# Causal mask of the exponentials: GpSimd selects in SBUF for TensorE mask matmuls, six casts moved to ScalarE, and a turn table written anew

## The chip, the cores and the metric

The kernel runs on 1 core of one Trainium2 chip. The metric is the device time of one execution in microseconds (us); the times of before are from 3 runs. TensorE is PE in the profile (PEld its weight loads), VectorE is DVE, ScalarE is ACT, GpSimd is POOL, and SP is the engine that issues most of the DMAs.

## What is computed

One transformer layer over 32 sequences (B) of 512 tokens (T) with 256 features, in float32: attention with rotary positions and a causal mask, then a mixture of experts. Cut to the attention that the change touches:

```python
q = (x @ Wq + bq).reshape(b, t, 16, 16).transpose(0, 2, 1, 3)      # 16 heads of 16
k = (x @ Wk + bk).reshape(b, t, 4, 16).transpose(0, 2, 1, 3)       # 4 groups, 4 heads each
v = (x @ Wv + bv).reshape(b, t, 4, 16).transpose(0, 2, 1, 3)
q, k = _rope(q), _rope(jnp.repeat(k, 4, axis=1)); v = jnp.repeat(v, 4, axis=1)
scores = jnp.einsum('bhtd,bhsd->bhts', q, k) / 4.0
scores = jnp.where(jnp.tril(jnp.ones((t, t), dtype=bool)), scores, -jnp.inf)
attn = jnp.einsum('bhts,bhsd->bhtd', jax.nn.softmax(scores, axis=-1), v)
out = attn.transpose(0, 2, 1, 3).reshape(b, t, 256) @ Wo + bo
```

Around it stand layer norms and residual sums. The second half routes each token to 2 of 16 experts (a gate of 16 outputs, top 2), adds a shared expert, and normalises again.

## The kernel before

The program has two phases. `attention_phase` does the attention, the gate and the routing of all 32 sequences and scatters each token's row to its experts' lists in DRAM; `expert_phases` then works through the 286 tiles of these lists and at last through the 32 sequences for the shared expert. The change is in the first phase alone.

The attention phase is a software pipeline over turns (`TURNS`, c from -3 to 33). In the turn c, sequence c has its exponentials and its weighing, c+1 has its first row maxima, c+2 its projections, its rotation and its splits, and c-1 and c-2 their output projection, norms, gate and routing. Within a turn everything has its place in a grid (g, e): four groups g of heads, and in each eleven units e of exponentials (`EXP_UNITS`). `turn_order()` walks this grid and puts next to every unit what the tables name there: `MAX_AT` and `SUMS_AT` place the maxima (step M) and the weighing (step P), `MISC` places steps of several engines, and `SIDE` places steps of one engine. Every engine walks the same list, takes its own steps from it and does them strictly in that order; semaphores tie the engines together.

Scores are made twice. For the maxima (`score_max`, L733), TensorE multiplies a query block by the keys up to the diagonal, with 96 rows in bfloat16: each float32 number is split into three bfloat16 parts, and the parts are stacked in `qs` and `ks`. A matmul of the identity with `mask_max` (L735) adds -3e38 above the diagonal, and VectorE takes the negated maximum of each row (L967). For the exponentials (`score_exp`, L749), TensorE multiplies keys by queries, with three more rows that subtract the maximum, and a matmul of the identity with `mask_exp` (L751) adds -3e38 to the 128x128 block on the diagonal, once for every head and key block. Units go through three PSUM buffers (`ps_a`). ScalarE takes the exponential of each unit into `probs` in SBUF (L856). `weigh` (L763) then multiplies them by the values and by ones, with all four heads of a group side by side in `ps_out`; key block j=0 and j=1 are weighed in the group itself, j=2 and j=3 in the next one. VectorE transposes the sums (L1005), inverts the denominators (L1007), and GpSimd divides (L677).

The splits of a sequence are GpSimd's: `split(b, unit, stage)` for unit 0 and 1 (the two halves of the queries) and 2 (the keys). Stage 0 forms the rotated number in `rest` (L598, L600, L602) from what VectorE left in `roped_q` (L979) and `roped_k`; stages 1 and 2 each round `rest` to a bfloat16 part (a cast written as an addition of zero, L594) and subtract that part (L596). There is one `rest`, so the units follow each other. When a unit is split, SP stores its three parts in DRAM (`store_parts`, L472), and when all are stored it loads them back as stacks, first the keys (L479) and then the queries of the four groups (L483), which `score_max` of the first group waits for in the next turn. The first sequence's splits are made by VectorE (`first_split`).

GpSimd also does three `root` steps a turn (eight small dependent operations each), two `split_max`, four `divide` and eight indirect DMAs that scatter rows (L666), all in one queue.

## Time and profile before

| | us |
|---|---|
| median of 3 runs | 2591.48 |
| lowest and highest | 2581.96, 2599.78 |
| profiled execution, its own time | 2595.59 |
| span of that execution (first to last instruction) | 2593.8 |
| attention phase, about | 0 to 1850 |
| expert tiles | 1855 to 2385 |
| shared expert and last norm | 2385 to 2594 |

The times below are from the profiled execution, and counted from its first instruction. A row of the timeline gives the start, the duration, the engine, the line and operation, output and inputs, and in brackets how long the engine had been idle and what ended that. A matmul's duration holds its way through the array, so two matmuls overlap, and what one costs is read from the distance between two starts. The values step (L881, one each sequence) is used as the mark of a turn: from one of its starts to the next.

### The profile page before, as it was taken

The page shows a single profiled execution, that of the slowest core. Times are in us where ns is not written, and L with a number is a line of the kernel's source. Part 1 is how long each engine was busy: PE and PEld are TensorE (multiplying, and loading weights), DVE is VectorE, ACT ScalarE, POOL GpSimd, SP SyncE. Part 2 cuts the span into 40 slices and gives each one's busy share as a digit, 9 for nine tenths or more (in the row PEclk, how much of TensorE's full clock was granted, in tenths as well). Part 3 has the DMA queues.
Part 4 walks back from the last instruction along what each step waited for, and adds up shares of the span by engine and source line. Part 5 has one row for each costly group of instructions (what it writes and reads, how often), then busy time and mean ns, then how long its engine had stood idle before and what let it go on. Part 6 is the DMA issues. An engine that isn't in the chain of part 4 may idle for free. (4 is left out here: it accounts for less than half of the span.)

```text
span 2593.8 us, 59479 instructions
## 1 busy us (share of the span) xinstructions
PE 2344.7 (90%) x18030; PEld 1507.9 (58%) x18030; DVE 2031.0 (78%) x5412; ACT 1396.6 (54%) x3228; POOL 1704.4 (66%) x2889
## 2 busy tenths in 40 slices
PE   4899999999999998899999999995389999999997
PEld 2555555555555555555555555553268877877664
DVE  5788888888887888788888878884357777776887
ACT  1455666556665665565666656564134444444664
POOL 2556767667766776677677667644266666766887
PEclk7899999999999998999999999997689999999999
DMA  4345444554455443455444453331356556554997
GB/s 126 89 135 148 128 130 148 155 150 134 131 156 159 128 130 111 124 151 163 139 128 136 137 155 116 115 116 58 81 153 182 155 148 198 162 150 147 318 348 243
DMA packets 288649, 387.93 MB, mean 150 GB/s; under 512 B 27922, under 2 KB 238098, under 8 KB 288212
## 3 DMA queue, kind: packets, MB, share of 16 engines
q1 hardware_dynamic: 260788, 308.56, 40.6%
q0 software_dynamic: 27552, 75.57, 8.6%
q8 instruction: 155, 2.54, 0.4%
q14 instruction: 154, 1.26, 0.2%
HBM read 193.40 MB, written 172.27 MB: 141 GB/s over the span
## 5 line engine op out<-in xcount | busy, mean ns | idle before, releaser
L856 ACT ACTIVATE probs<-ps_a 128x512 f32<-128x512 f32 (+1 forms) x1408 | 716.3, 560 | 519.0 <-PE ps_a L751 459.1
L967 DVE TENSOR_REDUCE negmax<-ps_d 128x2 f32<-128x768 f32 (+3 forms) x768 | 779.7, 1033 | 155.8 <-PE ps_d L735 142.3
L733 PE MATMUL ps_d<-ks,qs 96*128 96x128 bf16 (+3 forms) x2048 | 494.9, 308 | 97.0 <-DMA qs<-q_stack_dram 49.1
L749 PE MATMUL ps_a<-qs,ks 99*128 99x512 bf16 (+3 forms) x2048 | 526.3, 305 | 16.7 <-ACT probs L856 8.7
L735 PE MATMUL ps_d<-mask_max,ident_bf 128*128 128x128 bf16 x2048 | 401.3, 224 | 0.0
L751 PE MATMUL ps_a<-mask_exp,ident_bf 128*128 128x128 bf16 x2048 | 392.2, 221 | 0.0
L733 PEld LDWEIGHTS ps_d<-ks,qs 96*128 96x128 bf16 x2048 | 204.7, 100 | 267.5 <-issue 113.0
L1378 POOL DMA_INDIRECT y_dram<-ysb,to_row x286 | 282.4, 987 | 118.2 <-issue 81.5
L763 PE MATMUL ps_out<-probs,va 128*32 128x512 f32 (+3 forms) x4096 | 335.5, 446 | 0.2 <-ACT probs L856 0.2
L749 PEld LDWEIGHTS ps_a<-qs,ks 99*128 99x128 bf16 x2048 | 200.4, 98 | 217.1 <-issue 66.0
L1451 PE MATMUL ps_gu<-wgu,rows_t 128*128 x1144 | 305.7, 391 | 10.2 <-issue 6.7
L666 POOL DMA_INDIRECT sorted_dram<-h,slot x256 | 255.8, 999 | 65.8 <-issue 64.9
L1542 ACT ACTIVATE gate<-ps_gu 128x128 f32<-128x128 f32 x286 | 79.6, 278 | 269.2 <-issue 136.3
L751 PEld LDWEIGHTS ps_a<-mask_exp,ident_bf 128*128 128x128 bf16 x2048 | 202.8, 99 | 28.4 <-issue 21.5
L1451 PEld LDWEIGHTS ps_gu<-wgu,rows_t 128*128 128x128 f32 x1144 | 201.2, 196 | 29.0 <-issue 12.5
L735 PEld LDWEIGHTS ps_d<-mask_max,ident_bf 128*128 128x128 bf16 x2048 | 205.4, 100 | 0.4 <-issue 0.3
L1465 PE MATMUL ps_y<-wd,hid_t 128*128 x572 | 181.5, 399 | 19.0 <-ACT hid_t L1548 17.4
L763 PEld LDWEIGHTS ps_out<-probs,va 128*32 128x32 f32 x4096 | 108.1, 110 | 143.9 <-issue 74.7
L1611 DVE TENSOR_TENSOR hid<-ps_gu,gate 128x128 f32<-128x128 f32 x286 | 83.3, 291 | 117.4 <-ACT gate L1542 98.8
L205 POOL TENSOR_TENSOR pool_cell<-zero_col 1x1 f32<-1x1 f32 x318 | 58.7, 185 | 173.7 <-DVE slot L1101 111.9
L677 POOL TENSOR_TENSOR heads<-by_token,inverse 128x256 f32<-128x256 f32 x128 | 80.8, 631 | 135.5 <-DVE inverse L1007 129.4
L786 PE MATMUL ps_d<-wo,headst 128*128 128x256 f32 x512 | 148.2, 440 | 11.0 <-DVE place L1086 8.9
(196 smaller groups left out, 4447.4 us busy)
## 6 DMA issues: line engine op xcount, KB each, us to landing
qs<-q_stack_dram SPq DMA_DIRECT2D x128, 384.0 KB
rows<-sorted_dram SPq DMA_DIRECT2D x286, 129.0 KB
y_in<-y_dram SPq DMA_DIRECT2D x32, 1024.0 KB
q_stack_dram<-q_parts SPq DMA_DIRECT2D x64, 384.0 KB
x_in<-in_x SPq DMA_DIRECT2D x32, 512.0 KB
q_stack_dram<-q_parts SPq DMA_DIRECT2D x64, 256.0 KB
x<-in_x SPq DMA_DIRECT2D x32, 512.0 KB
h_dram<-h SPq DMA_DIRECT2D x32, 512.0 KB, 3.8
```

Source lines behind the costliest of these rows:

```text
L666: pool.indirect_dma_start(out=sorted_dram[b // (B // 2)][:, :], in_=h2[:, k, j, :], in_offset=None, out_offset=bass.IndirectOffsetOnAxis(a ...
L733: pe.matmul(ps_d[:, number % 2, at:at + width], qs[0:KR, b % 2, h, j * P:(j + 1) * P], ks[0:KR, b % 2, g, 0:width], start=True, stop=False)
L735: ins = pe.matmul(ps_d[:, number % 2, at + j * P:at + (j + 1) * P], ident_bf[:, :], mask_max[:, :], start=False, stop=True)
L749: pe.matmul(ps_a[:, number % 3, at:at + width], ks[0:KM, b % 2, g, j * P:(j + 1) * P], qs[0:KM, b % 2, g * HG + h0 + k, j * P:T], start=Tr ...
L751: ins = pe.matmul(ps_a[:, number % 3, at:at + P], ident_bf[:, :], mask_exp[:, :], start=False, stop=True)
L763: ins = pe.matmul(ps_out[32 * h:32 * h + 32, j * P:T], va[:, b % 3, j, g * 32:(g + 1) * 32], probs[:, at:at + width], start=(j == 0), stop ...
L786: ins = pe.matmul(ps[:, k * D:(k + 1) * D], headst[:, c, j * P:(j + 1) * P], wo[:, c, :], start=(c == 0), stop=(c == NC - 1))
L856: act.activation(probs[:, at:at + nh * width], ps_a[:, number % 3, 0:nh * width], ACT.Exp) \
L967: dve.tensor_reduce(negmax[:, g // 2, j, at:at + nh], src, AX_X, ALU.max, negate=True) \
L1378: pool.indirect_dma_start(out=y_dram[:, :], in_=ysb[:, k, :], in_offset=None, out_offset=bass.IndirectOffsetOnAxis(ap=to_row[k][:, 0:1].bi ...
L1451: ins = pe.matmul(ps_gu[:, t % 2, 0:2 * I], rows_t[:, t % 2, c, :], wgu[:, expert[t], c, :], start=(c == 0), stop=(c == NC - 1))
L1465: pe.matmul(ps_y[:, t % 2, 0:D], hid_t[:, t % 2, :], wd[:, expert[t], :], start=True, stop=True) \
```

## The change

`score_exp` no longer issues the mask matmul, and `mask_exp` is gone. In its place GpSimd gets a step `Z` for each group and key block, 16 in a turn: `triangle` waits until the last unit of that block has its exponentials, and sets to zero, in place in `probs`, the entries whose query stands before the key in the four heads' 128x128 diagonal blocks (one instruction over 4x128 columns). `weigh` waits for that step and not for the exponentials. In `split`, the six casts of a turn are taken from GpSimd and done by ScalarE as copies with rounding (`cast`); `rest` and the parts then pass from GpSimd to ScalarE and back by the same counting semaphore. The tables of the turn are new.

```diff
 MISC = {
     (0, 1): [("xt", 0, 2)],
-    (0, 8): [("W", 3, -1), ("R", 1, -1)],
-    (0, 9): [("cn", 0, -2)],
-    (1, 0): [("op", 0, -1)],
-    (1, 2): [("op", 1, -1)],
...
+    (0, 5): [("Z", 0, 0), ("T", 3, -1)],
+    (0, 6): [("Z", 15, -1), ("cn", 0, -2)],
...
+    (0, 10): [("op", 0, -1)],
+    (1, 0): [("op", 1, -1)],
+    (1, 1): [("Z", 3, 0)],
...
-MAX_AT = [[0, 0, 1, 4, 6, 10], [1, 2, 3, 6, 9, 9], [0, 2, 4, 5, 6, 8], [1, 2, 4, 7, 8, 9]]
-SUMS_AT = [10, 5]
+MAX_AT = [[0, 0, 1, 3, 9, 10], [3, 3, 5, 9, 9, 9], [0, 2, 3, 5, 8, 9], [2, 2, 5, 6, 7, 8]]
+SUMS_AT = [10, 4]
...
+    "cast0b": (1, 10),
+    "cast0c": (2, 1),
+    "cast1b": (3, 2),
+    "cast1c": (3, 4),
+    "cast2b": (3, 9),
+    "cast2c": (3, 10),
...
                 if stage or unit or b >= 1:
                     steps.settle()
-                if stage == 1 and unit == 0 and b >= 1:
-                    pool.wait_ge(parts_stored[(b - 1) % 2], PER_STORE * ((b - 1) // 2 + 1))
                 if stage:
                     k = stage - 1
-                    steps.did(pool.tensor_tensor(parts[k], r, zero_col[0:n, :].to_broadcast([n, T]), ALU.add))
-                    steps.settle()
                     steps.did(pool.tensor_tensor(parts[2] if k == 1 else r, r, parts[k], ALU.subtract))
...
+            def triangle(b, g, j):
+
+                pool.wait_ge(a_taken, A_NO["E", (g, LAST_OF_J[j]), b] + 1)
+                width = T - j * P
+                own = probs[:, PROBS_AT[j]:PROBS_AT[j] + HG * width].rearrange("p (h w) -> p h w", h=HG)[:, :, 0:P]
+                pool.affine_select(out=own, in_=own, compare_op=ALU.is_ge, fill=0.0, base=0,
+                                   pattern=[[0, HG], [1, P]], channel_multiplier=-1).then_inc(triangled, 1)
...
-                    pe.matmul(ps_a[:, number % 3, at:at + width], ks[0:KM, b % 2, g, j * P:(j + 1) * P],
-                              qs[0:KM, b % 2, g * HG + h0 + k, j * P:T], start=True, stop=False)
-                    ins = pe.matmul(ps_a[:, number % 3, at:at + P], ident_bf[:, :], mask_exp[:, :],
-                                    start=False, stop=True)
+                    ins = pe.matmul(ps_a[:, number % 3, at:at + width], ks[0:KM, b % 2, g, j * P:(j + 1) * P],
+                                    qs[0:KM, b % 2, g * HG + h0 + k, j * P:T], start=True, stop=True)
                 ins.then_inc(a_full, 1)
 
             def weigh(b, g, j):
 
-                pe.wait_ge(a_taken, A_NO["E", (g, LAST_OF_J[j]), b] + 1)
+                pe.wait_ge(triangled, Z_NO["Z", HG * g + j, b] + 1)
...
+            def cast(b, unit, k):
+
+                n = G * DH if unit == 2 else P
+                part = k_parts[:, k, :] if unit == 2 else q_parts[:, unit, k, :]
+                if unit == 0 and k == 0 and b >= 1:
+                    act.wait_ge(parts_stored[(b - 1) % 2], PER_STORE * ((b - 1) // 2 + 1))
+                act.wait_ge(split_steps, SPLITS * (3 * b + unit) + 2 * k + 1)
+                act.copy(part, rest[0:n, :]).then_inc(split_steps, 1)
```

The code of the changed kernel is some lines longer, so its lines have other numbers: 750 and 752 are the maxima's matmul and mask, 766 the exponentials' matmul, 801 the output projection, 603 the subtractions, 605, 607 and 609 the three `rest`, 616 the select, 692 the division, 909 the cast.

TensorE's queue of before, where a turn comes to the first maxima of the next sequence (group 0, ahead by one turn); L786 is the output projection:

```order
L786 MATMUL ps_d<-wo,headst 128x256 x4
L749 MATMUL ps_a<-qs,ks 128x512
L751 MATMUL ps_a<-mask_exp,ident_bf 128x128
L733 MATMUL ps_d<-ks,qs 128x128
L735 MATMUL ps_d<-mask_max,ident_bf 128x128
```

And of the changed kernel, at the same first maxima:

```order
L801 MATMUL ps_d<-wo,headst 128x256 x4
L766 MATMUL ps_a<-qs,ks 128x512
L801 MATMUL ps_d<-wo,headst 128x256 x4
L766 MATMUL ps_a<-qs,ks 128x512 x3
L750 MATMUL ps_d<-ks,qs 128x128
L752 MATMUL ps_d<-mask_max,ident_bf 128x128
```

In before, the first maxima come after one half of the output projection and one unit of exponentials, and the other half comes two sets of maxima later; now both halves and all four 512-wide units stand ahead of them. What follows is in both an ordinary row of maxima and units up to the query projection (L779, now L794).

GpSimd's queue of before, at the end of a sequence's splits (L594 and L596 on `k_parts` are the keys' casts and subtractions, L677 the division, L205 the wait for the scatter):

```order
L677 TENSOR_TENSOR heads<-by_token,inverse 128x16x16
L594 TENSOR_TENSOR k_parts_negmax_t<-rest,zero_col 64x512
L596 TENSOR_TENSOR rest<-rest,k_parts_negmax_t 64x512
L594 TENSOR_TENSOR k_parts_negmax_t<-rest,zero_col 64x512
L596 TENSOR_TENSOR k_parts_negmax_t<-rest,k_parts_negmax_t 64x512
L677 TENSOR_TENSOR heads<-by_token,inverse 128x16x16
L205 TENSOR_TENSOR pool_cell<-zero_col 1x1
```

And of the changed kernel, from the keys' `rest` on:

```order
L609 TENSOR_TENSOR rest<-roped_k_v_t 64x512
L616 AFFINE_SELECT probs<-probs 128x4x128
L692 TENSOR_TENSOR heads<-by_token,inverse 128x16x16
L603 TENSOR_TENSOR rest<-rest,k_parts_negmax_t 64x512
L603 TENSOR_TENSOR k_parts_negmax_t<-rest,k_parts_negmax_t 64x512
L616 AFFINE_SELECT probs<-probs 128x4x128 x2
L616 AFFINE_SELECT probs<-probs 128x512
L616 AFFINE_SELECT probs<-probs 128x4x128
L692 TENSOR_TENSOR heads<-by_token,inverse 128x16x16
L616 AFFINE_SELECT probs<-probs 128x4x128
L219 TENSOR_TENSOR pool_cell<-zero_col 1x1
```

The keys' casts are gone from this queue; one select stands inside the keys' split, and five stand behind it, ahead of the scatter, where before there was one division.

ScalarE's queue of the changed kernel at the same place (L883 to L891 are the gate's, L923 the norm of a sequence's input, L909 the casts of the keys):

```order
L883 ACTIVATE logits_t<-ps_a,act_bias 128x128
L871 ACTIVATE probs<-ps_a 128x384
L871 ACTIVATE probs<-ps_a 128x512 x2
L888 ACTIVATE gates<-ps_a 128x64
L891 ACTIVATE gates<-gates,act_bias 128x64
L909 CAST k_parts_negmax_t<-rest 64x512
L923 ACTIVATE h<-x_in,shift,rstd 128x256 x2
L871 ACTIVATE probs<-ps_a 128x512
L909 CAST k_parts_negmax_t<-rest 64x512
L923 ACTIVATE h<-x_in,shift,rstd 128x256 x2
```

In before the same stretch has no cast, and the four norms stand in one piece. Between the two casts of the keys there are now two norms and an exponential.

## Rows read from the trace of the kernel before

**Rows 1.** Busy time by stage: length, PE, PEld, DVE, ACT, POOL, clock, DMA share, GB/s.

```profile
200.00:1650.00 1450.00, 1368.57 (x12361) 813.33 (x12360) 1237.53 (x2881) 877.55 (x1806) 1013.09 (x1680) 0.98 0.47 138
1366.15:1418.42 52.27, 49.86 (x461) 29.55 (x459) 45.69 (x107) 32.56 (x68) 37.17 (x63) 1.00 0.47 138
1418.42:1472.62 54.20, 51.19 (x461) 30.75 (x459) 45.56 (x107) 32.56 (x68) 37.18 (x63) 0.97 0.44 133
973.37:1035.74 62.37, 55.28 (x461) 32.87 (x459) 53.53 (x137) 32.78 (x68) 40.21 (x64) 0.89 0.38 116
```

**Rows 2.** The values step of all sequences, from the view of its line.

```profile
L881 ACT COPY va<-ps_a x32: 372/378/379, 24.7 to 1689.5; 128x256 f32<-128x256 f32 x32
```

**Rows 3.** Timeline, TensorE: exponentials' matmuls and their masks.

```profile
1012.00 0.22 PE L749 MATMUL ps_a<-qs,ks 99*128 99x128 bf16 x1
1012.06 0.22 PE L751 MATMUL ps_a<-mask_exp,ident_bf 128*128 128x128 bf16 x1
1012.12 0.22 PE L749 MATMUL ps_a<-qs,ks 99*128 99x128 bf16 x1
```

**Rows 4.** Timeline: from first maxima over the splits to the next sequence's, and on.

```profile
1335.13 0.22 PE L733 MATMUL ps_d<-ks,qs 96*128 96x128 bf16 x1 [1.53 <-DMA qs<-q_stack_dram]
...
1347.04 1.27 POOL L598 TENSOR_TENSOR rest<-roped_q 128x512 f32<-128x512 f32 x1 [1.93 <-issue]
...
1375.74 1.15 POOL L596 TENSOR_TENSOR k_parts_negmax_t<-rest,k_parts_negmax_t 64x512 bf16<-64x512 f32 x1
1376.92 1.93 SPq L472 DMA_DIRECT2D k_stack_dram<-k_parts_negmax_t  x3
1380.70 0.34 SPq L479 DMA_DIRECT2D ks<-k_stack_dram  x1
1387.46 0.22 PE L733 MATMUL ps_d<-ks,qs 96*128 96x128 bf16 x1 [1.69 <-DMA qs<-q_stack_dram]
...
1388.88 1.98 PE L786 MATMUL ps_d<-wo,headst 128*128 128x256 f32 x8
...
1393.64 1.93 PE L779 MATMUL ps_d<-h1t,wq 128*128 128x512 f32 x4
```

**Rows 5.** Who waited for whom in the turn 1366.15 to 1418.42: GpSimd's waits (us, times, longest).

```profile
POOL heads L677 <- DVE inverse L1007: 3.8, 1, 3.8
POOL pool_cell L205 <- DVE slot L1101: 3.3, 1, 3.3
POOL rest L598 <- issue: 1.9, 1, 1.9
POOL var L632 <- issue: 0.8, 1, 0.8
```

**Rows 6.** Timeline, GpSimd: casts and subtractions of one unit.

```profile
1403.72 1.05 POOL L594 TENSOR_TENSOR q_parts<-rest,zero_col 128x512 bf16<-128x512 f32 x1
1404.85 1.17 POOL L596 TENSOR_TENSOR rest<-rest,q_parts 128x512 f32<-128x512 f32 x1
```

**Rows 7.** Timeline, GpSimd: selects over 128 columns, iotas over 16 and 512.

```profile
2.38 0.29 POOL L556 TENSOR_SCALAR_AFFINE_SELECT ident_bf<-ident_bf 128x128 bf16<-128x128 bf16 x1
2.63 0.29 POOL L559 TENSOR_SCALAR_AFFINE_SELECT mask_max<-mask_max 128x128 bf16<-128x128 bf16 x1
...
3.38 0.14 POOL L567 IOTA iota_e<- 128x16 f32 x1
...
1849.68 0.57 POOL L1367 IOTA own_row<- 128x512 f32 x1 [12.41 <-POOLq L336]
```

**Rows 8.** Groups of the whole span: a copy and the exponentials of ScalarE.

```profile
L885 ACT COPY h1t<-ps_a 128x512 f32<-128x512 f32 x64 | 37.6, 590 | 2.3 <-PE ps_a L803 2.3
L856 ACT ACTIVATE probs<-ps_a 128x512 f32<-128x512 f32 (+1 forms) x1408 | 716.3, 560 | 519.0 <-PE ps_a L751 459.1
```

**Rows 9.** GpSimd's cast, from the view of its line: shortest, median, longest in ns.

```profile
L594 POOL TENSOR_TENSOR q_parts<-rest,zero_col x124: 1032/1041/1367, 56.6 to 1688.6; 128x512 bf16<-128x512 f32 x124
```

More of the change, by code:

```diff
@@ L293, in layer @@
         mask_max = sb("mask_max", [P, P], BF16)
-        mask_exp = sb("mask_exp", [P, P], BF16)
         before = sb("before", [P, P], BF16)
@@ L325, in attention_phase @@
         v[n] for n in ("wq", "wkv", "bq", "bk", "rope", "wo", "bo", "gate_w", "act_bias", "wgu", "wd"))
-    (ident, ident_bf, mask_max, mask_exp, before, ones_bf, iota_e, token) = (
-        v[n] for n in ("ident", "ident_bf", "mask_max", "mask_exp", "before", "ones_bf", "iota_e", "token"))
+    (ident, ident_bf, mask_max, before, ones_bf, iota_e, token) = (
+        v[n] for n in ("ident", "ident_bf", "mask_max", "before", "ones_bf", "iota_e", "token"))
     (h2_std, h2_mean, counts, pool_cell, dve_cell, zero_col, tile_no, row_no) = (
@@ L560, in _ @@
                                base=0, pattern=[[-1, P]], channel_multiplier=1).then_inc(consts, 1)
-            pool.affine_select(out=mask_exp[:, :], in_=mask_exp[:, :], compare_op=ALU.is_ge, fill=MASKED,
-                               base=0, pattern=[[1, P]], channel_multiplier=-1).then_inc(consts, 1)
             pool.affine_select(out=before[:, :], in_=before[:, :], compare_op=ALU.is_ge, fill=1.0,
@@ L690, in _ @@
                         divide(b, arg)
+                    if step == "Z" and exists(b):
+                        triangle(b, arg // HG, arg % HG)
                     if step != "side":
@@ L907, in _ @@
                     if step == "side":
+                        if exists(c + 2) and c + 2 > 0:
+                            for unit in range(3):
+                                for k in range(2):
+                                    if at == SIDE[f"cast{unit}" + "bc"[k]]:
+                                        cast(c + 2, unit, k)
                         for part in range(2):
```

63 lines of the change are left out of this document (26 added, 37 removed), and 19 rows, old and new, of the table MISC.

## The prediction

> **What bounds the kernel now.** I read the busy time by stage first, then the timeline of one turn, then who waited for whom, and last the prices.
>
> The change is in the attention phase, whose turns run from one values step to the next: 31 intervals between 24.7 and 1689.5 us [rows 2]. A quiet turn is 52.27 us long and has TensorE at its full clock; another is 54.20 us at 0.97, and one of the two in which VectorE plans the experts' tiles is 62.37 us [rows 1]. In the quiet turn TensorE shows 49.9 us busy, VectorE 45.7, ScalarE 32.6 and GpSimd 37.2 [rows 1]. TensorE's figure says least: a matmul's record is 0.22 us long where the next starts after 0.06 [rows 3].
>
> So the reader should look for what makes TensorE stop. It stops once in every turn, at the first maxima of the next sequence, for the load of the query stacks: 1.53 us in one turn and 1.69 in the next [rows 4]. From there one can walk round a loop. First maxima at 1335.13; the query projection 6.2 us later (1387.46 to 1393.64 in the next turn); `rest`, when VectorE has rotated, at 1347.04, that is 5.7 us after the projection began; GpSimd's splits of queries and keys up to 1376.89 (29.8 us); SP's key store at once, the key load at 1380.70, and the first maxima again at 1387.46 (10.6 us) [rows 4]. The sum is 52.3 us, the turn itself. GpSimd waits for something 9.8 us in a turn, but all of it lies behind the keys' last subtraction and ahead of `rest` (the waits before the division, the scatter, the root and `rest` itself [rows 5]): inside its 29.8 us of the loop it never stops. The turn is set by this loop, and TensorE and VectorE are nearly as long.
>
> **The change part by part.**
>
> The mask matmuls. Matmul, mask and matmul start 0.06 us apart (1012.00, 1012.06, 1012.12 [rows 3]). There are 64 masks of the exponentials in a turn, so TensorE gets rid of 64 x 0.0585 = 3.7 us a turn, and of 2048 x 0.0585 = 120 us in all. That is the most that this part can bring, 125 us if the slower stretches are counted.
>
> GpSimd's queue. Its occupied time now is 52.3 - 9.8 = 42.5 us a turn. A cast and the wait behind it take 1.13 us (1403.72 to 1404.85 [rows 6]); six go: -6.7. Sixteen selects over 4x128 columns come, and no row shows one. A select over 128 columns takes 0.29 us, and two start 0.25 apart; an iota over 16 columns takes 0.14 us and one over 512 takes 0.57 [rows 7]. If the select has the short iota's fixed part of 0.13, its columns cost 0.157 us per 128, and one over 512 lasts 0.13 + 4 x 0.157 = 0.76 us and holds the queue for some 0.72. From below it is the long iota's 0.57 us (0.53 held), from above four times the short select's 0.29, 1.15 us (1.11 held). I take 0.72, since it rests on the select's own row; 16 x 0.72 = 11.5. For the second cast of the keys nothing stands between the two subtractions in GpSimd's queue, so GpSimd waits for ScalarE: 0.6 us for the cast and some 0.6 for what ScalarE is in the middle of, 1.2 in all. GpSimd then has 42.5 - 6.7 + 11.5 + 1.2 = 48.5 us (45.5 to 54.8 between the ends) of occupied time in a turn.
>
> The loop. From the first maxima to the query projection, half an output projection (1.8 to 2.0 us [rows 4]), two 512-wide units and a pair of maxima have been moved ahead of the maxima, and three masks are gone: 6.2 becomes about 3.2. Rotation stays at 5.7. In GpSimd's piece six casts go (-6.7), nine of the sixteen selects stand in it (9 x 0.72 = +6.5), and the wait for the last cast comes in (+1.2): 29.8 becomes 30.8. The stores and loads keep their 10.6, the same DMAs in the same order behind the same last subtraction. Sum: 3.2 + 5.7 + 30.8 + 10.6 = 50.3 us (48.6 and 53.8 with the select at its two ends). That is also what GpSimd's 48.5 needs, with some 1.8 us left for the waits which today are 9.8.
>
> ScalarE. A copy of 512 columns out of PSUM is 0.59 us [rows 8]; out of SBUF I take the same, 0.6, between half and twice that. Six are 3.6 us on an engine with 32.6 of 52.3 busy, and hide beside its waits for matmuls (459 us in the run, over 32 sequences some 14 a turn [rows 8]). But its queue is in order too. Behind a cast that waits for GpSimd stand exponentials, and behind these, three PSUM buffers later, TensorE. Where that cover is gone, a GpSimd that is late by 1 us makes TensorE late by nearly 1 us.
>
> The new wait of `weigh`. It waited for an exponential and now waits for a select behind whatever GpSimd has queued. The hardest place is key block 3 of group 0: its select stands behind the four scatters and a `split_max`. The counting step `cn` has been moved ahead by three units, so the scatters may start that much earlier, and the waits before the division and the scatter (3.8 and 3.3 us [rows 5]) are where the five added selects of that place go. I cost this at nothing; if that cover is gone the price is that of a select, 0.7 us, once or twice in a turn.
>
> The shared port. GpSimd's cast has a shortest time of 1032 ns, a median of 1041 and a longest of 1367 [rows 9]: in the middle case it loses 9 ns to anyone else. The Trainium skill ("SBUF — State Buffer", on the shared port pair) says that VectorE and GpSimd share a pair of SBUF ports and that whichever starts first keeps it for the whole instruction while the other is blocked. By that rule a select that meets one of VectorE's additions of two SBUF operands would stand still for up to that addition's length, and 16 selects give it 16 more chances; by the row such meetings are rare, and I add nothing. At the longest cast's excess of 0.33 us on every one of nine selects the loop would be 3 us longer, which is the case without gain below.
>
> The rest. The expert phases are untouched. The first three turns and the two of the planner are bounded otherwise and I give them the same gain, for want of a better row.
>
> The sum: 52.3 - 50.3 = 2.0 us, less a little, x 31 intervals = 60 us. The profiled execution took 2595.6 us (its span 2593.8) and would take 2535.6; the median of the runs is 4.1 lower, so the forecast is 2531.
>
> **The rivals.**
>
> Everything is gained. The loop gets its full relief because ScalarE's casts return in time and a select is as short as an iota, and the turn falls by all 3.7 us that TensorE loses: 2591.5 - 31 x 3.7 = 2477. For it speaks that VectorE's 45.7 us [rows 1] would fit into a turn of 48.6; against it that VectorE would then be busy 94% of the time, where it is now 87%, with the same two buffers between it and TensorE.
>
> No gain. The loop keeps its length, because each of the casts inside the splits comes back late (0.3 us more at six places is 1.8), or because selects are held up. Then TensorE's 3.7 us become waiting at the same place: 2580 to 2592, say 2586. For it speaks that the bound engine now is not the one that is relieved; against it the 3 us that were taken out between maxima and projection.
>
> The clock. Turns of 54.2 us have TensorE at a mean of 0.97 against 1.00 in the quiet ones of 52.3 [rows 1], and such a stretch follows the wait for the query stacks. About half of the turns have one. If TensorE, with 3.7 us less to do, idled more and every turn had one, some 14 more turns would lose 1.9 us each: 2531 + 27 = 2558. The Trainium skill ("TensorE: Matmul & The Clock Gate", the part on the oscillation) describes that: an idle TensorE has its clock halved until it has been busy again. The trace agrees in that the clock falls to the 1.2 GHz level after such a wait. Against it speaks that the first maxima now come later in the turn, so that this longest wait should shrink.
>
> Slower: GpSimd becomes the bound. Without its selects it has 37.0 us, and it can't do without some 1.3 us of waiting. With a held time s of one select the turn is 38.3 + 16 s, so it is as long as today's at s = 0.87 us; above that the kernel is slower. With s = 1.0, four short selects of 0.25 us one after the other, the turn is 54.3 and the time 2591.5 + 31 x 2.0 = 2654; at the upper end of 1.11 it is 56.1 and 2710. For it: a pattern of two dimensions in SBUF is in no row. Against: the per-column price would have to be that of the whole instruction.
>
> **How the numbers follow.** Chances: my forecast 0.45, everything gained 0.14, no gain 0.18, the clock 0.07, GpSimd the bound 0.16. The likeliest is 2531. The range is 2472 to 2625: down to the full gain and a little more, up into the case of a bound GpSimd, leaving out its dear half and some of the others' edges. Of 1% (26 us, about what a measurement of this kernel can tell from no change): faster by more holds the forecast but for its upper edge, the full gain and the clock, 0.65; within 1% the case without gain and that edge, 0.19; slower 0.16.
>
> **What would show it.** In the profile of the changed kernel: no line of `mask_exp`, and 64 matmuls fewer a turn; the select's group with a mean near 0.76 us (over 0.9 and the slower case is on); the distance of two values steps near 50.3 us in quiet turns; GpSimd with under 3 us of waits a turn; from the first maxima to the projection about 3.2 us; from `rest` of the first query half to the keys' last subtraction about 31. I am wrong if GpSimd still waits 6 us or more in a turn while the turn is 52, for then the loop is held elsewhere; or if TensorE's weight loads for `weigh` begin to wait for the selects by more than 1 us a turn, for then the new wait, which I cost at nothing, is the bound.

## The result: 6% slower, and the profile after

| | us |
|---|---|
| kernel before, median of 4 runs beside it | 2590.75 |
| changed kernel, median of 4 runs | 2745.47 (2741.59 to 2747.52) |
| ratio, 95% interval | 1.0595 [1.0557, 1.0634] |
| predicted | 2531 (2472 to 2625) |

The change costs 155 us where 60 less were forecast. The line of the values step dates the loss. It gives shortest, median and longest time in ns, then its first and last start:

```profile
L896 ACT COPY va<-ps_a x32: 372/372/373, 23.9 to 1827.3; 128x256 f32<-128x256 f32 x32
```

From first to last it is 1803.4 us, against 1664.8 before [rows 2]: 138.6 of the 146 us by which the spans differ. So all but a few of the lost microseconds lie in the turns of the attention phase. Two turns of the changed kernel, columns as in [rows 1]:

```profile
1536.86:1594.97 58.11, 48.83 (x396) 26.46 (x396) 45.69 (x107) 35.87 (x73) 40.66 (x72) 0.97 0.41 124
1594.97:1653.03 58.06, 48.79 (x396) 26.42 (x396) 45.73 (x107) 35.87 (x73) 40.64 (x72) 0.97 0.41 124
```

The turn has grown from 52.3 to 58.1 us and is nearly constant, but no engine has more than 49 us in it. VectorE's 45.7 is what it was; GpSimd is busy 40.6, so it isn't the bound by its load. A turn that is long, regular and full of gaps is held by waits. Who waited for whom, whole span:

```profile
ACT probs L871 <- PE ps_a L766: 431.1, 308, 5.7
PEld ps_out L778 <- POOL probs L616: 336.1, 210, 7.9
DVE negmax L996 <- PE ps_d L752: 308.6, 179, 10.3
PE ps_out L778 <- POOL probs L616: 233.2, 153, 7.6
POOL probs L616 <- ACT probs L871: 182.1, 102, 6.7
...
POOL rest L603 <- ACT q_parts L909: 96.7, 34, 3.9
```

TensorE waits 233 us for the selects, some 7 us a turn, in `weigh` (L778); before, its matmuls waited 0.2 us there in all, for exponentials. VectorE's wait for TensorE's maxima has more than doubled (142.3 before). On the other side the wait at the first maxima for the query stacks, which closed the loop that I walked [rows 4], is not among the waits any more. TensorE's waits for selects in the second of the two turns above (us, times, longest):

```profile
PE ps_out L778 <- POOL probs L616: 7.3, 5, 3.5
```

One place shows how it comes. This is the timeline of the changed kernel about group 2 of a turn; the columns are start, duration, engine, line and so on, as before:

```profile
1641.71 0.22 PE L752 MATMUL ps_d<-mask_max,ident_bf 128*128 128x128 bf16 x1
...
1642.92 0.64 POOL L616 TENSOR_SCALAR_AFFINE_SELECT probs<-probs 128x512 f32<-128x512 f32 x1
...
1643.48 1.23 DVE L996 TENSOR_REDUCE negmax<-ps_d 128x2 f32<-128x1024 f32 x1
...
1644.78 0.25 POOL L631 TENSOR_TENSOR negmax_parts<-negmax,zero_heads 128x32 bf16<-128x32 f32 x1 [0.64 <-DVE negmax L996]
...
1645.96 1.23 POOL L616 TENSOR_SCALAR_AFFINE_SELECT probs<-probs 128x512 f32<-128x512 f32 x2
1646.65 0.85 PE L778 MATMUL ps_out<-probs,va 128*32 128x384 f32 x8 [3.50 <-POOL probs L616]
...
1648.09 1.58 ACT L871 ACTIVATE probs<-ps_a 128x512 f32<-128x512 f32 x3 [3.00 <-PE ps_a L766]
1648.69 0.31 PE L750 MATMUL ps_d<-ks,qs 96*128 96x128 bf16 x1
1648.80 0.31 PE L752 MATMUL ps_d<-mask_max,ident_bf 128*128 128x128 bf16 x1
...
1649.79 0.69 DVE L996 TENSOR_REDUCE negmax<-ps_d 128x4 f32<-128x512 f32 x1 [4.47 <-PE ps_d L752]
...
1650.24 1.16 POOL L603 TENSOR_TENSOR rest<-rest,q_parts 128x512 f32<-128x512 f32 x1 [3.06 <-ACT q_parts L909]
```

Read it as a circle. TensorE issues the last maxima of the next sequence's group 1 at 1641.71. VectorE is then in the middle of the rotation of the keys, and reduces them from 1643.48 to 1644.71. GpSimd's `split_max` needs that reduction and starts at 1644.78. Behind `split_max` in GpSimd's queue stands the select of group 2, key block 1 (the first of the two at 1645.96), and TensorE's second weighing from there, which only some 1.2 us of other work parts from those very maxima, needs this select: it starts at 1646.65 after 3.50 us of idling. In that time TensorE feeds nobody: ScalarE then stands 3.00 us, VectorE 4.47, and GpSimd itself 3.06, since its next cast stands in ScalarE's queue behind the late exponentials. And TensorE comes back with matmuls that start 0.11 us apart (1648.69, 1648.80) where it is 0.06 at the full clock [rows 3]: it is at the lower of its two levels, 1.2 GHz, for a while. The select of 1642.92 belongs to key block 2, which is needed later: the two stand in the wrong order, with the division and `split_max` between them.

### The profile page after: what moved, and what is told of

The parts are those of the page before. It is cut to its first block and busy times, and to the rows that moved or that the text cites. A ratio compares the mean times of both kernels' runs of the same rounds, so it can differ in the third digit from the quotient of the medians.

```text
span 2739.9 us, 55925 instructions
## 1 busy us (share of the span) xinstructions
PE 2287.1 (83%) x15982; PEld 1385.0 (51%) x15982; DVE 2037.5 (74%) x5412; ACT 1497.6 (55%) x3414; POOL 1819.9 (66%) x3213
## 5 line engine op out<-in xcount | busy, mean ns | idle before, releaser
L778 PE MATMUL ps_out<-probs,va 128*32 128x512 f32 (+3 forms) x4096 | 362.9, 453 | 233.4 <-POOL probs L616 233.2
L750 PE MATMUL ps_d<-ks,qs 96*128 96x128 bf16 (+3 forms) x2048 | 510.1, 318 | 48.6 <-issue 19.1
L766 PE MATMUL ps_a<-qs,ks 99*128 99x512 bf16 (+3 forms) x2048 | 482.3, 315 | 14.8 <-ACT h1t L900 7.6
L616 POOL TENSOR_SCALAR_AFFINE_SELECT probs<-probs 128x512 f32<-128x512 f32 x512 | 323.4, 640 | 184.9 <-ACT probs L871 182.1
L752 PE MATMUL ps_d<-mask_max,ident_bf 128*128 128x128 bf16 x2048 | 418.0, 232 | 0.0
L778 PEld LDWEIGHTS ps_out<-probs,va 128*32 128x32 f32 x4096 | 96.1, 110 | 419.6 <-POOL probs L616 336.1
L766 PEld LDWEIGHTS ps_a<-qs,ks 99*128 99x128 bf16 x2048 | 172.6, 99 | 227.0 <-issue 113.5
L1633 DVE COPY rows_t<-ps_t 128x256 f32<-128x256 f32 x286 | 118.9, 416 | 43.9 <-PE ps_t L1468 36.0
L1661 DVE SCALAR_TENSOR_TENSOR ysb<-ps_y,rows,half_row 128x256 f32<-128x256 f32 x286 | 138.4, 484 | 9.4 <-remote 4.7
L1468 PE MATMUL ps_t<-ident,rows 128*128 128x128 f32 x572 | 112.1, 279 | 31.4 <-DMA rows<-sorted_dram 31.4
L801 PE MATMUL ps_d<-wo,headst 128*128 128x256 f32 x512 | 126.0, 390 | 14.4 <-DVE headst L1043 10.6
```

Of the source, the lines that this page charges most:

```text
L616: pool.affine_select(out=own, in_=own, compare_op=ALU.is_ge, fill=0.0, base=0, pattern=[[0, HG], [1, P]], channel_multiplier=-1).then_inc( ...
L750: pe.matmul(ps_d[:, number % 2, at:at + width], qs[0:KR, b % 2, h, j * P:(j + 1) * P], ks[0:KR, b % 2, g, 0:width], start=True, stop=False)
L752: ins = pe.matmul(ps_d[:, number % 2, at + j * P:at + (j + 1) * P], ident_bf[:, :], mask_max[:, :], start=False, stop=True)
L766: ins = pe.matmul(ps_a[:, number % 3, at:at + width], ks[0:KM, b % 2, g, j * P:(j + 1) * P], qs[0:KM, b % 2, g * HG + h0 + k, j * P:T], st ...
L778: ins = pe.matmul(ps_out[32 * h:32 * h + 32, j * P:T], va[:, b % 3, j, g * 32:(g + 1) * 32], probs[:, at:at + width], start=(j == 0), stop ...
L1468: ins = pe.transpose(ps_t[:, t % 2, c * P:(c + 1) * P], rows[:, t % RD, c * P:(c + 1) * P], ident[:, :])
```

## The experiments

Chips differ: the kernel before ran at 2585 to 2595 us beside some of these kernels and at 2557 to 2567 beside others. So kernels are compared by the ratio to before on their own chip, and "turn" is the median distance of two values steps in the profiled run. Absolute times in the expectations are for a chip on which before takes 2591. One and the same kernel, order_only and best_order below, came out at 0.9863 on one chip and at 0.9787 on another, so a difference of under a point between kernels of different chips says little.

### Is it the wait, the load, the casts or the order?

**a_no_select.** The changed kernel without its selects (the causal mask of the probabilities is left out).

```diff
-                    if step == "Z" and exists(b):
-                        triangle(b, arg // HG, arg % HG)
...
-                pe.wait_ge(triangled, Z_NO["Z", HG * g + j, b] + 1)
+                pe.wait_ge(a_taken, A_NO["E", (g, LAST_OF_J[j]), b] + 1)
```

> The changed kernel without its selects: weigh waits for the exponentials as in before, and neither mask matmul nor select is left, so the causal mask of the probabilities is left out. Theory W (weigh's new wait behind GpSimd's in-order queue closes a ring of waits through TensorE and ScalarE): the turn falls from 58.1 us to 49 to 51 and the time to 2470 to 2540. Theory C (the six casts in ScalarE's queue hold the ring): the time stays above 2690. Theory T (the new tables are bad by themselves): it stays above 2690.

Measured: ratio 0.986 [0.9775, 0.9946], turn 51.3 us. The selects with their wait cost the whole loss and more, 7.3 points.

**a_scratch.** The same (mask left out again), but GpSimd does two small dependent products at each select's place, and nobody waits for them.

```diff
-                width = T - j * P
-                own = probs[:, PROBS_AT[j]:PROBS_AT[j] + HG * width].rearrange("p (h w) -> p h w", h=HG)[:, :, 0:P]
-                pool.affine_select(out=own, in_=own, compare_op=ALU.is_ge, fill=0.0, base=0,
-                                   pattern=[[0, HG], [1, P]], channel_multiplier=-1).then_inc(triangled, 1)
+                number = 2 * Z_NO["Z", HG * g + j, b]
+                for k in range(2):
+                    pool.wait_ge(triangled, number + k + 1)
+                    pool.tensor_tensor(other[:, :], other[:, :], other[:, :], ALU.mult).then_inc(triangled, 1)
...
-                pe.wait_ge(triangled, Z_NO["Z", HG * g + j, b] + 1)
+                pe.wait_ge(a_taken, A_NO["E", (g, LAST_OF_J[j]), b] + 1)
```

> As a_no_select, but at each select's place GpSimd does, after the same wait for the exponential, two small dependent products on a tile of its own (about 0.6 us together, as long as a select is held), which nobody waits for. The causal mask of the probabilities is left out. Theory W (the wait of weigh is the cost): close to a_no_select, at most 40 us above it. Theory L (GpSimd's load, or its own new waits for ScalarE's exponentials, is the cost): near the changed kernel, above 2680.

Measured: 0.9911 [0.9885, 0.9938], turn 53.2. Two products take some 0.64 us, as one select does. GpSimd's load so costs some 0.5 points against a_no_select, with intervals that overlap. What is left, 6.8 of 7.3, comes with TensorE's wait.

**a_casts_pool.** The changed kernel with the six casts back on GpSimd.

```diff
+                    steps.did(pool.tensor_tensor(parts[k], r, zero_col[0:n, :].to_broadcast([n, T]), ALU.add))
+                    steps.settle()
...
-                                    if at == SIDE[f"cast{unit}" + "bc"[k]]:
-                                        cast(c + 2, unit, k)
```

> The changed kernel with the six casts back on GpSimd, its tables and its selects kept. Theory C (casts on ScalarE are the harm, GpSimd waits for them some 5 us a turn): falls below 2650. Theory W: GpSimd's queue gets 6.7 us longer and loses 5 us of waiting, so the selects come as late as before or later: 2740 to 2850.

Measured: 1.0993 [1.0902, 1.1084], turn 61.5. Moving the casts helps the changed kernel by 4 points.

**order_only.** The kernel before with the new tables `MISC`, `MAX_AT`, `SUMS_AT` and `SIDE` (entries for selects and casts have no effect there). Masks on TensorE, casts on GpSimd. Two of the tables:

```diff
-MAX_AT = [[0, 0, 1, 4, 6, 10], [1, 2, 3, 6, 9, 9], [0, 2, 4, 5, 6, 8], [1, 2, 4, 7, 8, 9]]
-SUMS_AT = [10, 5]
+MAX_AT = [[0, 0, 1, 3, 9, 10], [3, 3, 5, 9, 9, 9], [0, 2, 3, 5, 8, 9], [2, 2, 5, 6, 7, 8]]
+SUMS_AT = [10, 4]
```

> The kernel before with the tables of the changed one: mask matmuls on TensorE, casts on GpSimd, no selects, only the order of the turn is new. Theory T (the order is the harm): above 2690. Theory W and C: within 40 us of before, 2550 to 2630.

Measured: 0.9863 [0.9779, 0.9946], turn 51.6 where before's median is 53.5. The new order by itself is a gain, as large as that of a_no_select.

**b_no_mask.** The kernel before without the mask matmuls of the exponentials, the mask left out.

```diff
-                    pe.matmul(ps_a[:, number % 3, at:at + width], ks[0:KM, b % 2, g, j * P:(j + 1) * P],
-                              qs[0:KM, b % 2, g * HG + h0 + k, j * P:T], start=True, stop=False)
-                    ins = pe.matmul(ps_a[:, number % 3, at:at + P], ident_bf[:, :], mask_exp[:, :],
-                                    start=False, stop=True)
+                    ins = pe.matmul(ps_a[:, number % 3, at:at + width], ks[0:KM, b % 2, g, j * P:(j + 1) * P],
+                                    qs[0:KM, b % 2, g * HG + h0 + k, j * P:T], start=True, stop=True)
```

> The kernel before with the 64 mask matmuls of the exponentials in each turn simply left out, so the causal mask of the probabilities is left out; order, casts and waits as before. It prices what the masks cost TensorE there. Theory N (TensorE's mask time is not on the path: two kernels that differ only by these masks, with the new order, both had turns of 51.3 to 51.4 us): 2560 to 2592 us, turn 51.5 to 52.3. Theory M (the masks' 3.7 us a turn are fully on the path, as in my case of everything gained): 2460 to 2490 us, turn near 48.6.

Measured: 0.9992 [0.9965, 1.002]. TensorE's 2048 masks are worth nothing there. A turn, and the wait for the query stacks in the whole run, which was 49.1 us in 23 turns before:

```profile
1422.30:1474.77 52.47, 47.07 (x396) 25.69 (x395) 45.82 (x107) 32.68 (x69) 37.52 (x63) 1.00 0.46 137
```

```profile
PE ps_d L733 <- DMA qs<-q_stack_dram: 55.4, 25, 3.2
```

TensorE is busy 47.1 instead of 49.9 us in a turn as long as before, and the wait that closes the loop is longer by 6 us in the whole run. This is what one expects where a loop through other engines sets the turn.

**select_alone.** The kernel before with only the selects in place of the masks, each put behind its exponentials, casts on GpSimd. The first lines of what is added to before's `MISC`; the other groups are alike:

```diff
+    (0, 0): [("Z", 14, -1)],
-    (0, 1): [("xt", 0, 2)],
+    (0, 1): [("Z", 15, -1), ("xt", 0, 2)],
...
+    (0, 6): [("Z", 0, 0)],
...
-    (0, 9): [("cn", 0, -2)],
-    (1, 0): [("op", 0, -1)],
+    (0, 9): [("Z", 1, 0), ("cn", 0, -2)],
+    (1, 0): [("Z", 2, 0), ("op", 0, -1)],
+    (1, 1): [("Z", 3, 0)],
```

> The kernel before with the selects in place of the mask matmuls and nothing else: before's order of turns, the casts on GpSimd, each select put into GpSimd's order two or three units behind the last exponential that it needs. GpSimd would have 42.5 + 16 x 0.62 = 52.4 us of occupied time in a turn of 52.3. Theory W (weigh waiting for a select in GpSimd's in-order queue sets the turn): 2680 to 2850 us, with waits of TensorE for the selects of over 4 us a turn. Theory P (the selects only hurt at the places that the new order gave them): 2590 to 2640 us.

Measured: 1.0974 [1.0921, 1.1027], turn 61.9. Without the new order and the casts the selects cost nearly 10%. Theory P is out: the damage isn't tied to one table. In its turn GpSimd has 46.7 us busy, 6 more than in the changed kernel; how much of this loss is its load and how much TensorE's wait is not shown.

**order_casts.** The new order and the casts on ScalarE, masks on TensorE, no selects: the edit of a_no_select, and

```diff
-                    ins = pe.matmul(ps_a[:, number % 3, at:at + width], ks[0:KM, b % 2, g, j * P:(j + 1) * P],
-                                    qs[0:KM, b % 2, g * HG + h0 + k, j * P:T], start=True, stop=True)
+                    pe.matmul(ps_a[:, number % 3, at:at + width], ks[0:KM, b % 2, g, j * P:(j + 1) * P],
+                              qs[0:KM, b % 2, g * HG + h0 + k, j * P:T], start=True, stop=False)
+                    ins = pe.matmul(ps_a[:, number % 3, at:at + P], ident_bf[:, :], mask_exp[:, :],
+                                    start=False, stop=True)
```

> The changed kernel with the masks back as TensorE matmuls and without the selects: the new order and the six casts on ScalarE alone. weigh waits for the exponentials. The new order alone took 2549 us with a turn of 51.4. Theory G (GpSimd's piece of the loop still sets the turn there, so 6.7 us less casts on it shorten the turn): 2480 to 2525 us. Theory V (with the new order VectorE, 46 of 51 us busy, and its hand-over with TensorE are the bound, and the casts bring nothing more): 2535 to 2560 us.

Measured: 0.9922 [0.9896, 0.9947], turn 52.5. A turn of it:

```profile
1404.72:1457.20 52.48, 49.58 (x460) 29.83 (x459) 47.02 (x108) 35.58 (x75) 30.90 (x57) 1.00 0.45 137
```

GpSimd is down to 30.9 us busy in a turn, and it is no faster than the order alone. The casts help only a GpSimd that has the selects too. Theory G is out: with the new order the loop through GpSimd's splits doesn't set the turn any more. That VectorE, 47.0 of 52.5 us busy, does is what theory V says and fits the time, but no run made VectorE's work shorter.

### Which place

**after_swap.** The changed kernel with two pairs of selects exchanged in `MISC`; the rows (1, 3) and (1, 6) are the edit of group 1, the rows (2, 8) and (3, 1) that of group 2.

```diff
-    (1, 3): [("Z", 5, 0)],
+    (1, 3): [("Z", 4, 0)],
-    (1, 6): [("Z", 4, 0), ("T", 0, 0), ("qe", 0, 2), ("qe", 1, 2)],
+    (1, 6): [("Z", 5, 0), ("T", 0, 0), ("qe", 0, 2), ("qe", 1, 2)],
-    (2, 8): [("Z", 10, 0), ("kk", 0, 2), ("W", 1, 0)],
+    (2, 8): [("Z", 9, 0), ("kk", 0, 2), ("W", 1, 0)],
-    (3, 1): [("Z", 9, 0)],
+    (3, 1): [("Z", 10, 0)],
```

> The changed kernel with two pairs of selects exchanged in GpSimd's order: those of group 1, key blocks 0 and 1, and those of group 2, key blocks 1 and 2. In the changed kernel the later-needed one stands first in each pair and waits for its exponentials while the other, whose exponentials are done and which TensorE waits for, stands behind it. If this head-of-line waiting makes the ring long: 2600 to 2700 us. If the length of GpSimd's queue ahead of the select (root, splits, division) is what matters and not these two places: 2730 to 2750 us.

Measured: 1.0023 [1.0005, 1.0042], turn 53.5. Four entries exchanged in a table give back nearly all of the 6%.

**swap_g1** and **swap_g2**, each with the edit of one group.

> The changed kernel with only one pair of selects exchanged in GpSimd's order: group 1, key blocks 0 and 1. Both pairs exchanged took 2601 us against 2745. Theory R (one ring: the place by group 2 sets the turn, since the chain of waits walked in the changed kernel goes through group 2's block 1 and not through this one): 2720 to 2750 us. Theory S (each inversion costs half by itself): 2665 to 2680 us.

> The changed kernel with only the other pair exchanged: group 2, key blocks 1 and 2. Theory R (this place carries the ring): 2601 to 2640 us. Theory S (each inversion costs half): 2665 to 2680 us.

Measured: group 1 alone 1.0525 [1.0475, 1.0575], turn 57.9; group 2 alone 0.99 [0.9855, 0.9945], turn 52.2. It is group 2, and that by more than theory R gave it (the 0.7 points of group 1 lie within overlapping intervals): with its one pair exchanged the changed kernel is faster than the kernel before. (The exchange in group 1 then costs 1.2% again; what it does was not followed up.) The same place in swap_g2:

```profile
1442.06 0.22 PE L752 MATMUL ps_d<-mask_max,ident_bf 128*128 128x128 bf16 x1
...
1443.47 0.63 POOL L616 TENSOR_SCALAR_AFFINE_SELECT probs<-probs 128x512 f32<-128x512 f32 x1
1443.83 1.22 DVE L996 TENSOR_REDUCE negmax<-ps_d 128x2 f32<-128x1024 f32 x1
...
1444.15 0.85 PE L778 MATMUL ps_out<-probs,va 128*32 128x384 f32 x8 [0.65 <-POOL probs L616]
...
1445.13 0.25 POOL L631 TENSOR_TENSOR negmax_parts<-negmax,zero_heads 128x32 bf16<-128x32 f32 x1 [0.45 <-DVE negmax L996]
...
1445.59 0.22 PE L750 MATMUL ps_d<-ks,qs 96*128 96x128 bf16 x1
1445.65 0.22 PE L752 MATMUL ps_d<-mask_max,ident_bf 128*128 128x128 bf16 x1
```

```profile
1396.78:1448.94 52.16, 46.67 (x396) 25.64 (x396) 45.77 (x107) 35.58 (x74) 40.40 (x73) 1.00 0.46 138
```

The select now runs beside VectorE's reduction instead of behind it; TensorE stops for 0.65 us, comes back with matmuls 0.06 us apart, and its clock is at 1.00 for the turn. The work of VectorE, ScalarE and GpSimd is within 0.3 us of the changed kernel's; the turn is 5.9 us shorter.

**z9_ahead_max** and **z9_behind_max** part the two things that the exchange mends at once: that the select stood behind `split_max`, and that it stood behind the select of block 2.

```diff
 z9_ahead_max:
-    (2, 8): [("Z", 10, 0), ("kk", 0, 2), ("W", 1, 0)],
+    (2, 8): [("Z", 10, 0), ("kk", 0, 2), ("W", 1, 0), ("Z", 9, 0)],
-    (3, 1): [("Z", 9, 0)],
 z9_behind_max:
-    (2, 8): [("Z", 10, 0), ("kk", 0, 2), ("W", 1, 0)],
+    (2, 8): [("kk", 0, 2), ("W", 1, 0)],
+    (2, 10): [("Z", 9, 0)],
-    (3, 1): [("Z", 9, 0)],
+    (3, 1): [("Z", 10, 0)],
```

> The changed kernel with one select moved: that of group 2, key block 1, from behind split_max to just ahead of it, still behind the select of key block 2 and the division. Theory F (a forced round trip: TensorE's last maxima of group 1, VectorE's reduction of them, split_max, this select, and TensorE's weighing, which stands right behind those maxima, so TensorE must stop for its whole length whatever the slack): the turn falls from 58.1 to 52 to 53 us, ratio to the kernel before 0.985 to 1.005. Theory I (what counts is that it stands behind the select of block 2, whose exponentials come later): the turn stays at 57 to 58 us, ratio 1.04 to 1.06.

> The changed kernel with the selects of group 2 in their natural order, block 1 and then block 2, but both behind split_max. Theory F (the round trip through split_max): turn 57 to 58 us, ratio 1.045 to 1.06, with the wait of TensorE for this select some 3 us. Theory I (the inverted pair): turn 52 to 53.5 us, ratio 0.985 to 1.005.

Measured: ahead of `split_max` 1.0168 [1.0121, 1.0214], turn 54.6; in natural order but behind `split_max` 1.0549 [1.0498, 1.0601], turn 58.0. The weighing of that block in each, first z9_ahead_max:

```profile
1450.90 0.85 PE L777 MATMUL ps_out<-probs,va 128*32 128x384 f32 x8 [1.99 <-POOL probs L615]
```

And z9_behind_max:

```profile
1464.07 1.51 PE L779 MATMUL ps_out<-probs,va 128*32 128x384 f32 x8 [3.51 <-POOL probs L617]
```

Behind `split_max` the stop is 3.51 us, as in the changed kernel, though the selects are in order: the round trip of theory F is there, and theory I doesn't explain the turn of 58. But order isn't nothing either: ahead of `split_max` and behind one more select and the division, the stop is 1.99 us, and the kernel lands above the interval that F gave. Of the 7 points between 1.0595 and 0.99, the place behind `split_max` is worth 4.3 and the two other instructions ahead 2.7.

z9_ahead_max also prices the clock. Two of its turns, one after the other, with 5.9 us of stops for selects in each:

```profile
1455.69:1509.60 53.91, 46.61 (x396) 25.67 (x396) 45.80 (x107) 35.68 (x73) 40.98 (x73) 1.00 0.45 134
1509.60:1565.09 55.49, 48.20 (x396) 26.44 (x396) 45.80 (x107) 35.78 (x73) 41.36 (x73) 0.97 0.45 130
```

The turn with a stretch at the lower level is 1.6 us longer, and TensorE is busy 1.6 us more in it.

### What is left, and the best version

**swap_three** is after_swap with the select of group 3, block 3, ahead of the next sequence's first as well, and **swap_three_p5** also weighs blocks 2 and 3 one unit later.

```diff
-    (0, 5): [("Z", 0, 0), ("T", 3, -1)],
-    (0, 6): [("Z", 15, -1), ("cn", 0, -2)],
+    (0, 5): [("Z", 15, -1), ("T", 3, -1)],
+    (0, 6): [("Z", 0, 0), ("cn", 0, -2)],
 swap_three_p5, and g2_p5 below:
-SUMS_AT = [10, 4]
+SUMS_AT = [10, 5]
```

> Both pairs exchanged and a third of the same kind: the select of group 3, key block 3, ahead of that of the next sequence's first block, behind which it stands and which waits 1.6 us for its exponentials while TensorE waits 1.2 us for the block 3. Theory H (every wait of TensorE for a select that stands behind one that can't start yet is on the path): 2560 to 2585 us. Theory E (with the two exchanged the rest is even between the engines and the third brings nothing): 2595 to 2603 us.

> The three exchanges, and the weighing of each group's key blocks 2 and 3 one unit later in TensorE's order (5 in place of 4, where the kernel before had it), so that their selects, which TensorE waits 1.2 us for in one turn at block 2 of group 1, have 3 us more. Theory H (TensorE's waits for selects are what is left): 2550 to 2580 us, below the kernel with three exchanges by 10 or more. Theory E (no gain left there): within 6 us of the kernel with three exchanges.

Measured: 0.993 [0.9903, 0.9956] and 0.9909 [0.988, 0.9937], turns 52.9 and 52.3. Both start from after_swap at 1.0023 and gain on it; against swap_g2 neither is a gain, and between the two the intervals overlap. Inconclusive.

**g2_casts_pool.** swap_g2 with the casts back on GpSimd, the edit of a_casts_pool.

> The changed kernel with the pair of group 2 exchanged (0.990 of before) and the six casts back on GpSimd. With the round trip in place the casts on GpSimd cost 96 us. Theory Q (GpSimd's queue is long in any case: 40.7 us of instructions and 6.7 more): ratio 1.01 to 1.05, turn 53.5 to 56. Theory O (the casts cost only because they lengthened the round trip and what followed it): ratio 0.985 to 1.0, turn 52 to 52.6.

Measured: 1.0573 [1.0527, 1.062], turn 58.0, above both theories. A turn of it:

```profile
1479.76:1537.76 58.00, 47.51 (x396) 26.22 (x396) 47.37 (x107) 33.05 (x68) 47.11 (x79) 0.97 0.43 124
```

GpSimd has 47.1 us in 58.0. At the place in group 2 TensorE's stop stays short (0.61 us in the turn before this one), and it stops for selects at other places instead:

```profile
1466.27 1.25 PE L780 MATMUL ps_out<-probs,va 128*32 128x256 f32 x16 [2.08 <-POOL probs L618]
...
1488.47 0.85 PE L780 MATMUL ps_out<-probs,va 128*32 128x384 f32 x8 [3.02 <-POOL probs L618]
```

So the casts are worth 6.7 points to this kernel and 4.0 to the changed one. It fits that every microsecond in GpSimd's queue can stand ahead of one of sixteen selects for which TensorE waits. But GpSimd waits for other engines only 5.7 us in this turn, where in the changed kernel it does so for 12.9: how much of the 6.7 points is its load, and how much the places of the instructions, is not shown.

**g2_p5**, swap_g2 with the later weighing (diff above), then the same kernel as **best_selects** beside the new order alone, **best_order**, on one chip:

> The changed kernel with the pair of group 2 exchanged, and the weighing of each group's blocks 2 and 3 one unit later in TensorE's order. In the kernel with three exchanges this took the turn from 52.9 to 52.3 and the ratio from 0.993 to 0.991. If TensorE's waits of some 0.4 us for selects at those places are on the path: turn 51.5 to 52, ratio 0.980 to 0.987. If not: ratio 0.988 to 0.993, as with the exchange alone.

> The same kernel as g2_p5 (selects, casts on ScalarE, one pair exchanged, weighing one unit later), timed again beside best_order on one chip. If the selects and the casts bring something beyond the new order: a ratio lower than that of best_order by over 0.003. If the order alone is the gain: both at 0.984 to 0.988.

> The same kernel as order_only (masks on TensorE, casts on GpSimd, the new order alone). Its quiet turn was 51.4 us where the kernel with selects and casts has 52.2. Ratio 0.984 to 0.988 if it is as good as best_selects, or better.

Measured: g2_p5 0.9857 [0.9813, 0.9901]; then best_selects 0.9858 [0.9829, 0.9887] (2525 us against 2560), and best_order 0.9787 [0.976, 0.9814] (2508). The version to take is the kernel before with the new tables and nothing else, 2.1% faster on this chip (1.4% in order_only, two runs on another). Mended, the selects and casts still lose 0.7% to it. A turn of best_order, and of best_selects:

```profile
1378.04:1429.45 51.41, 49.55 (x460) 29.83 (x460) 46.21 (x107) 33.03 (x68) 37.31 (x63) 1.00 0.46 140
```

```profile
1441.84:1494.02 52.18, 46.87 (x396) 25.61 (x395) 45.91 (x107) 35.61 (x74) 40.38 (x74) 1.00 0.48 139
```

The one with 2.7 us less TensorE and 3.1 us more GpSimd has the longer turn. In best_order the waits for selects don't exist; in best_selects TensorE still waits 78 us in the run for them:

```profile
PE ps_out L778 <- POOL probs L616: 77.9, 120, 7.7
```

## Why the prediction was wrong

**The bound and the loop: right for the kernel before, not for the new order.** The forecast said that TensorE's figure said least and that a loop over the stacks sets the turn. b_no_mask bears it out: 2.8 us less TensorE in a turn, no gain, a longer wait for the stacks. In order_only, with the maxima moved, that wait is gone from the profile. (No run made GpSimd's piece of the loop shorter in the old order, which would have been the other half of the proof.) But the forecast went on to add up the changed kernel's turn from the same loop, 50.3 us, as if nothing else could hold it. In order_only the 6.2 us from first maxima to projection are 3.35 (1467.76 to 1471.11), 2.8 us out of the loop, and the quiet turn went from 52.3 to only 51.4, and six casts less on GpSimd brought nothing more (order_casts, 52.5): under the new order something else holds the turn first. Even with the selects' waits mended the 50.3 isn't reached; swap_g2 has 52.2. The step "6.2 becomes about 3.2" measured 3.2 us (first maxima 1619.62, query projection 1622.81).

**The price of a select: forecast too dear.**

```profile
L616 POOL TENSOR_SCALAR_AFFINE_SELECT probs<-probs x512: 624/635/758, 80.5 to 1932.4; 128x512 f32<-128x512 f32 x171
```

0.64 us instead of 0.76. Sixteen are 10.2 us of busy time, and the slower rival, a GpSimd that is the bound by its load, needed 0.87 held: it didn't happen. The time fell on the slower side, which had a chance of 0.16, but by another mechanism than the one that this chance was given to. The span of GpSimd's splits, from `rest` to the keys' last subtraction, was forecast at 31 and is 34.6 us: the 3.06 us wait for a cast lies in it. GpSimd's waits for other engines, forecast at under 3 us in a turn, are 12.9.

**The casts: size right.** They take 0.62 us on ScalarE (0.6 forecast). That a late GpSimd makes TensorE late by way of the casts in ScalarE's queue is not shown: the casts' waits for GpSimd, but for the first of all, are 51.5 us in the run, under 2 us a turn, and no run tells whether any of it reaches TensorE. The 3.06 us are the opposite, GpSimd waiting for a cast behind exponentials that TensorE had delayed.

**The new wait of weigh: the step that failed.** I wrote: "I cost this at nothing; if that cover is gone the price is that of a select, 0.7 us, once or twice in a turn." Measured: 7.3 us of TensorE's waits in a turn, 3.50 of them at one place. (The sum of the waits is not their price: a turn of swap_g2 has 4.0 us of them, and that kernel is faster than before. The 1 us of such waits that the forecast took as its sign of being wrong was too low a mark.) Two things were wrong. I looked at one select only, the one behind the scatters in group 0, and not at where each of the sixteen stands against its weighing. And I priced a lost cover by the instruction waited for. The price is the length of everything between: 1.55 us until VectorE has done the rotation that stands ahead in its queue, 1.23 of reduction, 1.2 of `split_max` in four steps, 0.63 of select. From the last maxima's end at 1641.93 to the select's end, some 0.63 us after 1645.96, that is 4.7 us, and TensorE's stop is this less the 1.2 us of its own work in between. More slack elsewhere in the turn can't hide it, because the way begins with TensorE's own last instructions. The 3.50 us against swap_g2's 0.65 are 2.85 of the 5.9 us a turn. The clock, at a mean of 0.97 against 1.00 in swap_g2, accounts for some 1.6 more, by the two turns of z9_ahead_max. Of the remaining 1.4 us, 0.4 to 0.5 are longer stops for the other selects (3.8 against 3.35 us); the rest wasn't taken apart.

**The clock rival** described a thing that happens, with the wrong trigger: the clock does fall in each of these turns, after the wait for the select and not for the stacks. The Trainium skill ("TensorE: Matmul & The Clock Gate", the part on the oscillation) has an engine that idled come back at half its clock. By that rule the stop of `weigh` should do the same, and the trace agrees: starts 0.11 us apart behind the stop of 3.50 us, 0.06 behind the one of 0.65 us.

**What the forecast took as the gain** was the order's alone. Its 2.0 us a turn came from moving the maxima, and order_only has 0.9 of it in a quiet turn and 1.9 in the median one, with every mask still on TensorE. The forecast never priced the parts of the change against each other. Masks off TensorE: nothing in the old order, and in the new one 0.6 points between order_casts and a_no_select, on two chips and with intervals that overlap. Selects: a loss. Casts: help only against the selects.

## What to carry to other kernels

Before work moves to another engine's in-order queue, list for each new wait what stands ahead of the awaited instruction in that queue, and follow each of those back: where one comes back to something that the waiting engine issued only just before, the way round is a stop that slack elsewhere doesn't hide, and it is priced by its whole length, queues included, less what the engine itself does meanwhile. One select moved behind the division and a step that waits for TensorE's newest result turned a gain of 1% into a loss of 5.5% (swap_g2 and z9_behind_max). And where a change comes with a new order, run the order alone: it may be all the gain there is.

## What the runs showed that I had not expected

Two chips, or one chip at two times, differ by 1.5% for the same kernel (before: 2595 and 2557 us), and most of it can lie outside the attention phase: from the first load of an expert's rows to the end of the span it is 735.8 us in order_only (2549.5 - 1813.7) and 710.2 us in best_order (2509.3 - 1799.1), the very same kernel. That is 25.6 of the 40.2 us between the two spans. Ratios taken on one chip are what can be compared.

A strided select over 4x128 float32 columns in SBUF costs GpSimd 0.64 us, near the 0.57 us of an iota of the same width [rows 7] and far from four times the 0.29 us of a select over 128 bfloat16 columns: in this kernel one instruction over four heads is much cheaper than four, and the pattern's second dimension shows no price of its own.
